# Order of work in the third convolution's attention loop, and of gelus and routing in the second experts

## The reference, cut to what matters

```python
# second experts (B=4 images, S=256 tokens, D=64, E=8 experts, F=128)
logits = mean(x, axis=1) @ Wr + br                   # one row for each image
routing_weights = softmax(logits)
expected_loads = routing_weights.sum(axis=0) * (N / B)
scale = where(expected_loads > capacity, capacity / expected_loads, 1.0)
routing_weights = softmax(routing_weights * scale)
top_w, top_i = top_k(routing_weights, 2); top_w = softmax(top_w)
h = gelu(einsum('nd,edf->enf', xf, W1) + b1)         # all experts, all tokens
y = einsum('enf,efd->end', h, W2) + b2
out = layer_norm(einsum('ne,end->nd', w_dense, y) + x, gamma, beta)

# third convolution (heads g=8, head size 16)
q, k, v = split(conv3x3(x, w_qkv))
attn = einsum('bgnd,bgmd->bgnm', q, k) / (qn * kn + 1e-4)
attn = attn * pb                                     # pb = exp(-scale * distance), rows normed
out = einsum('bgnm,bgmd->bgnd', attn, v)
out = relu(batch_norm(conv1x1(out, w_out)))
```

## Time and profile before

| | |
|---|---|
| median of 3 runs | 771.08 us (768.73 to 773.09) |
| profiled execution | 772.89 us, span 771.1 us |
| busy in the span | PE 589.8, DVE 501.7, ACT 377.9, POOL 278.0 us |
| mean granted TensorE clock | 0.826 of 2.4 GHz |
| second experts, from first to last instruction | 309.3 to 358.2 us of the span |
| third convolution | 358.7 us on; its loop's last `result` ends at 471.5 |

### The profile page before, as it was taken

The page is one execution under the profiler, slowest core; times in us unless marked ns, Lnnn a source line. Parts: engine busy times, 40 slices in busy tenths (PEclk is TensorE's granted clock), DMA queues, the critical chain, the costliest instruction groups (busy, mean ns, idle before and its releaser), DMA issues. The chain is left out here.

```text
span 771.1 us, 8274 instructions
## 1 busy us (share of the span) xinstructions
PE 589.8 (76%) x2469; PEld 353.7 (46%) x2469; DVE 501.7 (65%) x1226; ACT 377.9 (49%) x568; POOL 278.0 (36%) x219
## 2 busy tenths in 40 slices
PE   4663879999995698482997775599875997988781
PEld 2563657777773484261444442433533534751110
DVE  2772566777775653666954654882287893849986
ACT  3002647888873740252536652364023245939852
POOL 4998357788784100301005760500012382000000
PEclk9997689999997799576998557599579798569995
DMA  3441000000000500402000000300021000000000
GB/s 107 114 119 45 1 1 1 0 1 1 0 2 13 101 0 1 154 1 79 7 1 0 1 1 1 84 1 0 1 64 28 0 2 8 1 0 0 0 0 14
DMA packets 18516, 18.44 MB, mean 24 GB/s; under 512 B 10954, under 2 KB 14347, under 8 KB 18088
## 3 DMA queue, kind: packets, MB, share of 16 engines
q1 hardware_dynamic: 18472, 17.93, 8.9%
HBM read 17.02 MB, written 0.26 MB: 22 GB/s over the span
## 5 line engine op out<-in xcount | busy, mean ns | idle before, releaser
L646 POOL TENSOR_TENSOR l0f_hid_lo<-l0f_hid,l0f_hid_hi 114x512 fp32r<-114x512 f32 (+1 forms) x75 | 98.0, 1317 | 48.6 <-ACT l0f_hid_hi L728 47.8
L824 DVE TENSOR_TENSOR l0f_hid<-l0f_silu,PS 114x512 f32<-114x512 f32 x96 | 65.7, 687 | 41.8 <-ACT l0f_silu L745 40.7
L682 PE MATMUL PS<-l0f_xs,l0w_hi 128*114 128x512 f32 x192 | 78.6, 409 | 0.0
L682 PE MATMUL PS<-l0f_xs,l0w_lo 128*114 128x512 f32 x192 | 77.5, 403 | 0.0
L745 ACT ACTIVATE l0f_silu<-PS 114x512 f32<-114x512 f32 x96 | 57.7, 602 | 31.9 <-PE PS L682 31.2
L2530 PE MATMUL PS<-l3f_ring,l3f_slots 128*32 128x512 f32 x128 | 54.9, 647 | 13.0 <-DVE l3f_ring L2611 13.0
L728 ACT CAST l0f_hid_hi<-l0f_hid 114x512 fp32r<-114x512 f32 x96 | 59.1, 615 | 2.9 <-DVE l0f_hid L824 2.3
L1325 POOL TENSOR_TENSOR l2c_den<-l2c_far,l2c_den 128x1024 f32<-128x1024 f32 x16 | 37.6, 2358 | 63.2 <-ACT l2c_den L1483 63.2
L2611 DVE SCALAR_TENSOR_TENSOR l3f_ring<-l3f_ring,l_countT 128x1024 f32<-128x1024 f32 x32 | 39.0, 1226 | 10.4 <-ACT l3f_ring L2561 10.4
L2557 ACT ACTIVATE l3f_ring<-l3r_plain,l3r_neg 128x1024 f32<-128x1024 f32 x32 | 36.0, 1134 | 11.9 <-PE PS L2530 11.9
L2605 DVE SCALAR_TENSOR_TENSOR l3f_ring<-l3f_slope,l3r_low,l3f_ring 128x1024 f32<-128x1024 f32 x32 | 40.9, 1285 | 0.4 <-ACT l3f_ring L2557 0.4
(11 more groups left out here) (581 smaller groups left out, 1327.2 us busy)
## 6 DMA issues: line engine op xcount, KB each, us to landing
l0w_raw<-in_l_w SPq DMA_DIRECT2D x32, 170.5 KB, 3.2
l3k_edge<-in_edges SPq DMA_DIRECT2D x2, 1024.0 KB
l2c_wqkv<-in_l_wqkv SPq DMA_DIRECT2D x3, 384.0 KB, 4.3
l0w_w<-in_l_w SPq DMA_DIRECT2D x8, 142.5 KB
l2f_raw<-in_l_w SPq DMA_DIRECT2D x2, 512.0 KB, 6.2
l1c_pos_w<-in_l_pos_w SPq DMA_DIRECT2D x1, 784.0 KB, 4.7
l1c_vrow<-l1c_vimg SPq DMA_DIRECT2D x7, 88.0 KB, 4.0
l1f_raw<-in_l_w SPq DMA_DIRECT2D x2, 256.0 KB
```

The lines of the kernel that those rows point to most:

```text
L646: g.tensor_tensor(hid_lo[0:k, q % HIDS, :], hid[0:k, q % HIDS, :], hid_hi[0:k, q % HIDS, :], ALU.subtract).then_inc(S("low_pool"), 1)
L682: last = t.matmul(m.PS[0:k, (one, two)[z], :], half[:, e, z, a:a + k], xs[:, h * HALF:(h + 1) * HALF], start=(half is ew.hi), stop=(half i ...
L824: v.tensor_tensor(hid[0:k, at % HIDS, :], silu[0:k, at % RING0, :], m.PS[0:k, two, :], ALU.mult).then_inc(S("free"), 1)
```

## The change

Second experts: ACT casts each half straight from PSUM to `xs` (`high_scalar`), DVE writes the rest of the split by halves (`low_vector`) and makes the mean from PSUM by halves. `up` runs five banks deep. Three more `up` (`early`) follow behind `load` on PE, and ACT does three gelus between the first and the second exponential; the other 13 follow the third exponential, with the copy of `gateT` after the ninth gelu. On PE the remaining eight `up` stand behind `gate_wide`, ahead of the two `b2` matmuls. The zero matmuls go; the down products go image by image, bank 0 and bank 6, so that ACT can take the first one while PE makes the second. The root's table is loaded by an extra root before `b2g`. The norm at the end uses bn_stats and bn_aggr, multiplies with gamma before the reciprocal, and beta is added to `X` earlier (`Xb`).

Third convolution: on ACT `weight(u+1)` moves ahead of the logarithm that stood between; on DVE both products of a pair are back to back.

```diff
-        bank = lambda j: (2, 3, 1, 7)[j % 4]
+        deep, early = 5, 3
+        bank = lambda j: (2, 3, 1, 7, 5)[j % deep]
...
-            g.memset(zero[:], 0.0).then_inc(S("zero"), 1)
...
-            norm_tensor(t, m)
-            t.wait_ge(S("zero"), 1)
-            t.matmul(m.PS[:, 0, :], zero[:, 0:P], zero[:], start=True, stop=False, skip_group_check=True)
+            turn_tensor(t, m)
             t.wait_ge(S("w"), 16 * nw)
             t.wait_ge(S("mean"), 1)
             t.matmul(m.PS[0:B, 4, 0:E1], mean[:], wr[:], start=True, stop=True).then_inc(S("logits"), 1)
-            t.wait_ge(S("xs"), 2)
-            for j in range(4):
+            for j in range(deep):
+                t.wait_ge(S("xs"), min(j, 1) + 1)
                 up(j)
             t.wait_ge(S("soft"), 1)
             t.matmul(m.PS[0:B, 4, 0:E1], ones[:], rt[:, 0, 0:E1], start=True, stop=True).then_inc(S("load"), 1)
+            for j in range(deep, deep + early):
+                up(j)
             t.wait_ge(S("gate"), 1)
...
             last.then_inc(S("gate_wide"), 1)
+            for j in range(deep + early, len(steps)):
+                up(j)
             t.wait_ge(S("gateT"), 1)
...
-            for j in range(4, len(steps)):
-                up(j)
-            t.wait_ge(S("w2g"), 1)
-
-            for j, (h, e) in enumerate(steps):
-                t.wait_ge(S("hid"), j + 1)
-                for s in range(2):
-                    t.matmul(m.PS[h * C:(h + 1) * C, 0, s * N:(s + 1) * N], w2g[:, 2 * h + s, e, :], hid[:, j, s * N:(s + 1) * N],
-                             start=False, stop=False, skip_group_check=True)
-            t.matmul(m.PS[:, 0, :], zero[:, 0:P], zero[:], start=False, stop=True, skip_group_check=True).then_inc(S("down"), 1)
+
+            for s in range(2):
+                for j, (h, e) in enumerate(steps):
+                    if j < 2:
+                        t.wait_ge(S("w2g"), 2 * s + h + 1)
+                    t.wait_ge(S("hid"), j + 1)
+                    last = t.matmul(m.PS[h * C:(h + 1) * C, (0, 6)[s], 0:N], w2g[:, 2 * h + s, e, :], hid[:, j, s * N:(s + 1) * N],
+                                    start=(e == 0), stop=True, skip_group_check=True)
+                last.then_inc(S("down"), 1)
...
-            norm_scalar(a, m)
-            a.wait_ge(m.sem("norm_xt"), 2 * m.norms + 2)
-            a.copy(xs[0:C, :], m.XT[0:C, :]).then_inc(S("xs"), 1)
+            high_scalar(a, m, xs)
             softmax_scalar(a, m, rt[:, :, 0:E1], "l1f", 1)
+            for j in range(early):
+                gelu(j)
             softmax_scalar(a, m, rt[:, :, 0:E1], "l1f", 2)
             a.wait_ge(S("less_top"), 1)
             a.activation(rt[:, 0, 0:E1], rt[:, 0, 0:E1], ACT.Exp).then_inc(S("top_exp"), 1)
-            a.wait_ge(S("gate_wide"), 1)
-            a.copy(gateT[:], m.PS[0:E1, 4, 0:B]).then_inc(S("gateT"), 1)
+            for j in range(early, len(steps)):
+                gelu(j)
+                if j == 8:
+                    a.wait_ge(S("gate_wide"), 1)
+                    a.copy(gateT[:], m.PS[0:E1, 4, 0:B]).then_inc(S("gateT"), 1)
+            a.activation(m.stat[:, 2, :], m.stat[:, 2, :], ACT.Sqrt)
...
-            for j in range(len(steps)):
-                gelu(j)
             a.wait_ge(S("down"), 1)
-            for s in range(2):
-                ins = a.activation(m.Y2[:, s * N:(s + 1) * N], m.PS[:, 0, s * N:(s + 1) * N], ACT.Identity, bias=b2g[:, s:s + 1])
-                ins.then_inc(m.sem("y_ready"), 1) if s else m.act_step(a, ins)
+            a.activation(m.Y2[:, 0:N], m.PS[:, 0, 0:N], ACT.Identity, bias=b2g[:, 0:1]).then_inc(S("first_half"), 1)
+            a.wait_ge(S("down"), 2)
+            a.wait_ge(S("first_half"), 1)
+            a.activation(m.Y2[:, N:2 * N], m.PS[:, 6, 0:N], ACT.Identity, bias=b2g[:, 1:2]).then_inc(m.sem("y_ready"), 1)
...
+            for h in range(2):
+                v.wait_ge(m.sem("norm_xt"), 2 * m.norms + h + 1)
+                do(v.tensor_reduce(mean[:, 2 * h:2 * h + 2], m.PS[0:C, h, :].rearrange("c (b n) -> c b n", b=2), AX.X, ALU.add))
+            v.tensor_scalar(mean[:], mean[:], 1.0 / N, None, ALU.mult).then_inc(S("mean"), 1)
+            for h in range(2):
+                low_vector(v, m, xs, h, S("xs"))
...
+            do(v.tensor_tensor(Xb[:], m.X[:], lnw[:, 1:2, :].broadcast_to([P, NB, C]), ALU.add))
             codes.code_vector(v)
...
-            do(v.tensor_reduce(mean8, R[:], AX.X, ALU.add))
-            do(v.tensor_scalar(mean8, mean8, 1.0 / C, None, ALU.mult))
-            do(v.tensor_tensor(R[:], R[:], over(mean8, full), ALU.subtract))
-            do(v.tensor_tensor(m.sq[:], R[:], R[:], ALU.mult))
-            do(v.tensor_reduce(var8, m.sq[:], AX.X, ALU.add))
-            v.tensor_scalar(var8, var8, 1.0 / C, 1e-5, ALU.mult, ALU.add).then_inc(S("var"), 1)
+            for j in range(NB):
+                m.dve_step.go_on(v.bn_stats(moments[:, j, 0:6], R[:, j, :]))
+            v.wait_ge(m.dve_step.sem, m.dve_step.n)
+            for j in range(NB):
+                m.dve_step.go_on(v.bn_aggr(moments[:, j, 6:8], moments[:, j, 0:6]))
+            v.wait_ge(m.dve_step.sem, m.dve_step.n)
+            v.tensor_scalar(var8.unsqueeze(2), moments[:, :, 7:8], 1e-5, None, ALU.add).then_inc(S("var"), 1)
+            do(v.tensor_tensor(R[:], R[:], moments[:, :, 6:7].broadcast_to(full), ALU.subtract))
+            do(v.tensor_tensor(R[:], R[:], lnw[:, 0:1, :].broadcast_to(full), ALU.mult))
             v.wait_ge(S("dev"), 1)
             do(v.reciprocal(rdev8, dev8))
             do(v.tensor_tensor(R[:], R[:], over(rdev8, full), ALU.mult))
-            do(v.tensor_tensor(R[:], R[:], lnw[:, 0:1, :].broadcast_to(full), ALU.mult))
-            do(v.tensor_tensor(R[:], R[:], lnw[:, 1:2, :].broadcast_to(full), ALU.add))
-            do(v.tensor_tensor(m.X[:], m.X[:], R[:], ALU.add))
+            do(v.tensor_tensor(m.X[:], Xb[:], R[:], ALU.add))
@@ third convolution, ACT @@
             for u in range(3):
                 log(u)
-            for u in range(n):
+            weight(0)
+            for u in range(1, n):
                 weight(u)
-                if u + 3 < n:
-                    log(u + 3)
+                if u + 2 < n:
+                    log(u + 2)
@@ third convolution, DVE @@
             for k in range(len(quads)):
                 attention(2 * k)
+                attention(2 * k + 1)
+                codes.next_vector(v, range(4 * k, 4 * k + 4))
                 if k:
                     result(k - 1)
-                codes.next_vector(v, range(4 * k, 4 * k + 4))
-                attention(2 * k + 1)
                 codes.ends_vector(v, range(4 * k, 4 * k + 4), codes.late)
```

More of the change, by code:

```diff
@@ L1082, in l1_ffn_stage @@
         xs = sb("xs", [2 * C, T], F32R)
-        zeros, zero = sb("zeros", [2 * C, 2]), sb("zero", [1, HALF])
+        zeros = sb("zeros", [2 * C, 2])
         w2, b2 = sb("w2", [F1, E1, C]), sb("b2", [E1, C])
@@ L1095, in l1_ffn_stage @@
         b2g = sb("b2g", [2 * C, B // 2])
-        R = sb("R", [P, NB, C])
+        R, Xb, moments = sb("R", [P, NB, C]), sb("Xb", [P, NB, C]), sb("moments", [P, NB, 8])
         S = lambda name: m.sem("l1f_" + name)
@@ L1130, in up @@
                 t.wait_ge(S("split"), e // (E1 // 2) + 1)
-                if j >= 4:
-                    t.wait_ge(S("hid"), j - 3)
+                if j >= deep:
+                    t.wait_ge(S("hid"), j - deep + 1)
                 for part in (hi, lo):
@@ L1150, in _ @@
             for b in range(B):
-                last = t.matmul(m.PS[:, 5, b * E1:(b + 1) * E1], pickb[:, b, :], rt[:, 0, 0:E1], start=True, stop=True)
+                last = t.matmul(m.PS[:, 0, b * E1:(b + 1) * E1], pickb[:, b, :], rt[:, 0, 0:E1], start=True, stop=True)
             last.then_inc(S("gate_wide"), 1)
+            for j in range(deep + early, len(steps)):
+                up(j)
             t.wait_ge(S("gateT"), 1)
             for h in range(2):
-                last = t.matmul(m.PS[h * C:(h + 1) * C, 6, 0:B // 2], b2[:], gateT[:, 2 * h:2 * h + 2], start=True, stop=True)
+                last = t.matmul(m.PS[h * C:(h + 1) * C, 4, 0:B // 2], b2[:], gateT[:, 2 * h:2 * h + 2], start=True, stop=True)
             last.then_inc(S("b2g"), 1)
-            for j in range(4, len(steps)):
-                up(j)
-            t.wait_ge(S("w2g"), 1)
-            for j, (h, e) in enumerate(steps):
-                t.wait_ge(S("hid"), j + 1)
-                for s in range(2):
-                    t.matmul(m.PS[h * C:(h + 1) * C, 0, s * N:(s + 1) * N], w2g[:, 2 * h + s, e, :], hid[:, j, s * N:(s + 1) * N],
-                             start=False, stop=False, skip_group_check=True)
-            t.matmul(m.PS[:, 0, :], zero[:, 0:P], zero[:], start=False, stop=True, skip_group_check=True).then_inc(S("down"), 1)
+            for s in range(2):
[6 more added lines that the diff above has]
+                last.then_inc(S("down"), 1)
             back_tensor(t, m, stacked=True)
@@ L1182, in _ @@
```

(25 more changed lines are left out.)

## The result

Changed kernel: median 745.78 us (741.36 to 746.72, 4 runs), against 770.05 for the kernel before in the same series; ratio 0.9668, interval 0.9619 to 0.9718. A second series, further down, gave 745.53 and 0.9635 (0.9600 to 0.9671). The ratios make the gain 25.6 and 28.2 us; 21.6 was forecast. The direction and the places were right.

The account below looks back on a forecast made before the run. A ring of waits was taken to bound the loop, latency the second experts; 13.6 (loop) + 6.3 (experts) + 1.7 (normalisation) = 21.6 us, giving 749.5 us against the median, with 745 to 756 holding 8 in 10.

Parts of the forecast that it names:

- What bounds it: Both changed stages: a ring of waits sets the loop's period, latency the second experts; no engine is full.
- Loop, DVE order and ACT order: Third convolution's loop: back-to-back products cut DVE's ring to 4.8 us; ACT's second exponential is ready 1.5 us early.
- Loop, PE as the bound at 5.2: Third convolution's loop: at the slow clock PE bounds the period at 5.2 us; 5.0 taken, six periods gain 11.8.
- rival A: Third convolution's loop: a full PE keeps the clock at 2.4 GHz; period 4.7, time 747 us; chance 0.14.
- Tail of the loop: Third convolution, last scores to last result: 8.1 us becomes 7.2, a gain of 0.8 us.
- Second experts, head to downs: Second experts up to DVE's first norm sum: that sum starts 6.3 us earlier (5 to 7.2).
- DVE as the next bound: Second experts: if the clock rises sooner, DVE's weights, Xb and edge coding bound the stage; gain 7.2 us.
- Table switches: Second experts, ACT: a table switch costs 1.3 us in all, against 2.66 by the Trainium skill.
- Normalisation: End of the second experts: the norm takes 5.7 us against 7.4, a gain of 1.7 us.
- B: Second experts gain only 4 us: switches delay the second exponential, or downs begin at 1.2 GHz; 753.5 us; chance 0.12.
- C: Loop keeps its period, the wait moving to ACT; only the second experts' 8 us remain; 763 us; chance 0.07.
- D: Loop slower: logarithm held behind a weight, POOL runs dry, 13.8 us a period; 804 us; chance 0.04.

Follow-up runs that it names:

- the two halves: Kernel before with DVE's loop order alone: 763.0 us, ratio 0.9880; kernel before with ACT's loop order alone: 773.1 us, ratio 1.0011.
- filler_after: Changed kernel with two more 256-column matmuls on PE at the end of each loop period; 744.5 us, ratio 0.9641.
- pool_half: Changed kernel with the subtraction in POOL's exponent left out for half of each element's columns; 743.35 us, one run.
- no_early: Changed kernel without the three early gelus and the three pairs of matmuls behind load; 748.0 us, ratio 0.9679.
- experts_only: Kernel before with the edits of the second experts alone; 762.7 us, ratio 0.9866.

## Why the prediction was right in kind and too small

- *What bounds it.* Right: both stages behaved as chains, and the rest of the kernel didn't change (0.6 us).
- *Loop, DVE order and ACT order.* Right, and shown by the two halves: alone 1.2 a period and nothing, together 2.36. The wait that would have come is the 1.10 for ACT. The slack of 1.5 us that I gave the second exponential isn't there, though: its exponent comes from a full POOL, and in two of the six periods the second product waits 0.37 and 0.42 for ACT. I had named "no wait of DVE for ACT" as a sign.
- *Loop, PE as the bound at 5.2.* This is the first of the two steps that failed: "5.1, or 5.2 with a gap", so "at the slow clock PE becomes the bound". I added PE's groups one behind the other (2.44 + 1.87 + 0.79), from rows in which the second `sums` and the next `scores` had been kept apart by a wait. In the changed kernel's slow period they come to 2.52 + 1.87 + 0.35 = 4.74: the next `scores` begin 0.35 after the second `sums` begin, not 0.79. And they begin 0.06 to 0.07 behind DVE's second product there and in `pool_half`'s slow period (4.73), so what these periods measure is DVE's ring, which I had right at "4.8" and then passed over for PE's sum. POOL's I took as 4.7 from single exponents of 2.37; in a row they have a pitch of 2.33, 4.66 a period. So both ends of "4.7 and 5.2" were really 4.7, and the middle, 5.0, was 0.4 too long: six periods make 2.3 us.
- *The clock in the loop.* I weighed it as what decides between 4.7 and 5.2 (rival A). It rose in part (0.82), yet it isn't the cause of the miss: `filler_after` has it at 1.00 in five of the six periods and gains nothing. What it does explain is the kernel before, where at 1.00 it is worth 1.94 of 6.96 us.
- *Tail of the loop.* 1.3 instead of 0.8. `values` of the last pair ran at the fast clock, 1.07 instead of 1.94, where I had 2.0; the last products gave 0.4 of it back by waiting for ACT.
- *Second experts, head to downs.* Forecast 6.3, measured 8.8, and this is the second step that failed: I kept the clock at 1.2 GHz until the downs ("7.2 at the fast clock at which they ran"), so the gate matmuls and the eight pairs stood in the sum at their slow durations. The clock was up from 320.9 to 327.7 and again from 331.1. The terms that were mis-sized: `load` 1.1 earlier instead of 0.3, of which 0.2 is the stage's start; the gate matmuls 1.03 instead of 1.85, so that the gate was done at 327.6 and not at 329.1; the eight pairs 5.4 instead of 6.9; the weights 2.50 instead of 2.87. Gate (1.5) and pairs (1.5) make up the 3.0 us by which DVE's sum started before the 344.9 of PE's path in my sum. In `no_early`, with the five pairs but nothing behind them, the clock was up from 322.0 to 325.5, while PE had nothing to do, and down at the gate. With the early pairs it was still up when the gate came, in `experts_only` only in part (1.53), and there the gain was 7.4 and not 8.8. Whether the early pairs hold it over the wait, or it only rose at another moment, these few profiles don't separate.
- *DVE as the next bound.* Right in kind: I had it as the limit if the clock rises sooner, at 7.2 of gain. With the gate done 1.5 sooner and the weights 0.4 shorter than in that sum it gave 8.8 (7.4 in `experts_only`, where PE was the later one), and DVE's coding and PE's result now end within 0.1 us of each other.
- *Table switches.* 318.99 to 320.28: 1.29 from the load's start to the gelu. The load pushed the second exponential back by 0.1 only (input ready at 323.31, load done at 323.43, start at 323.44). The rule of the Trainium skill ("ScalarE: Activation LUTs", What ACT_TABLE_LOAD costs) of a drain of 1.38 us at each switch isn't what these traces show, in three switches in which the next work was ready when the load ended.
- *Normalisation.* 5.73 against a forecast of 5.7.

Rivals B, C and D are out: the experts' part gave more, not half; there was 0 to 0.4 of waiting for ACT in the loop; POOL never ran dry, it ran full.

## What to carry to other kernels

When a ring is cut, the new period is the largest of the engines' own sums, or of a shorter ring that is left, and these have to be taken from stretches where the groups really run back to back: read from rows with a wait between them, PE came out at 5.1 where 4.74 was enough. A busy engine isn't yet the bound; look at what the next group's start follows. An order edit on one engine often needs its partner on another; alone ACT's gave nothing and DVE's half. Where a loop shows a low granted clock with PE idle for part of each period, try a few matmuls in the gap before redesigning the order: here that gave 10.7 of the 14.1 us that six periods gained. Two of them at the start of each stage took another 0.6% off, with intervals that just touch.

## What the runs showed of the hardware that I had not expected

- `sums` (4 rows by 128 columns) and `scores` (32 rows by 128 columns) overlap on PE where nothing keeps them apart: in the changed kernel `scores` begin at 414.90, 0.35 after the first of the `sums` and 0.03 before the last two of them. PE's groups of a slow period fit into 4.74, against 5.10 added up from the rows of the kernel before.
- Matmuls whose result nobody reads raised the granted clock of the old loop from 0.53 to 1.00 (0.96 over the six periods with the first one) and kept it there for five periods, with PE still idle for part of each.
- In the changed kernel the clock stayed at 1.00 from 323.2 to 326.6 while PE had nothing to do, and fell to 0.50 at 327.7, just behind the gate matmuls.
- POOL's exponents at half the columns take 1.28 instead of 2.36, somewhat more than half.
